# Product-key stages: combining on POOL behind an ACT copy, outputs moved behind the products

## The reference

```
def _L1_ffn_ref(inputs, gamma, beta, w_q, keys, key_in, key_out):   # h=8 heads, nk=32, top 8
    xn = (x - mu) * rsqrt(var + eps) * gamma + beta                  # over all tokens
    q = xn @ w_q.T                                                   # two halves a head
    sim = einsum('pbnhd,hkpd->pbnhk', q, keys)                       # 32 scores a half
    s, i = top_k(sim, 8); all_scores = sx[..., :, None] + sy[..., None, :]
    scores, pk = top_k(all_scores, 8)                                # 8 of 1024 experts a head
    o = einsum('bnd,bnhkd->bnhk', inputs, key_in[idx])
    o = gelu(o) * softmax(scores)
    return einsum('bnhk,bnhkd->bnd', o, key_out[idx])
```

## Time and profile before

| | us |
|---|---|
| median of 3 runs | 1822.73 (1818.83 to 1823.32) |
| the profiled execution | 1822.42 |
| its span | 1820.6 |
| PE busy | 1531.7 (84%) |
| PE weight loads busy | 1234.6 (68%) |
| DVE busy | 1350.5 (74%) |
| ACT busy | 933.3 (51%) |
| POOL busy | 243.7 (13%) |

### The profile page before, as it was taken

How to read it: one execution, slowest core, us unless ns; L and a number is a source line. 1 busy time by engine, 2 the same in 40 slices (tenths; PEclk the granted TensorE clock), 3 DMA queues, 4 the chain that set the end, 5 groups by cost and what they waited for, 6 DMA issues and landing times.

```text
span 1820.6 us, 58068 instructions
## 1 busy us (share of the span) xinstructions
PE 1531.7 (84%) x22876; PEld 1234.6 (68%) x22876; DVE 1350.5 (74%) x4272; ACT 933.3 (51%) x1990; POOL 243.7 (13%) x389
## 2 busy tenths in 40 slices
PE   2767777777579999999986899999958999999995
PEld 1644444445458888888874677777736888888885
DVE  4956666667689999999954556556568899999992
ACT  1814454447375666766722223323336667667670
POOL 2136455432000000000002000000000000000000
PEclk9958898887799999999987899999969999999997
DMA  5000000000011112112110000000001121121212
GB/s 135 1 1 1 1 0 0 0 1 1 0 25 43 40 35 46 35 35 46 35 36 1 1 1 0 0 0 0 0 0 37 36 46 35 36 44 35 45 36 71
DMA packets 27503, 42.67 MB, mean 23 GB/s; under 512 B 6960, under 2 KB 18480, under 8 KB 27440
## 3 DMA queue, kind: packets, MB, share of 16 engines
q1 hardware_dynamic: 27440, 41.82, 10.1%
HBM read 6.15 MB, written 2.10 MB: 5 GB/s over the span
## 4 chain that ended last, share of the span: by engine, by line
PE 48%; DVE 20%; issue 11%; DMA 7%; ACT 5%; SPq 5%; DVEq 2%; POOL 1%; POOLq 0%; ACTq 0%; PEldq 0%
PE bank L1518 19%; DMA rowsD<-work 7%; SPq L305 5%; DVE work L858 4%; DVE work L852 4%; ACT work L941 3%; PE bank L1393 3%; PE bank L1381 3%; PE bank L1430 3%; PE bank L1241 3%; PE bank L1529 2%; PE bank L1165 1%; PE bank L1403 1%; DVE work L582 1%; PE bank L1184 1%
## 5 line engine op out<-in xcount | busy, mean ns | idle before, releaser
L1518 PE MATMUL bank<-rowsD,work 128*32 128x32 f32 x16384 | 366.3, 273 | 48.1 <-DMA rowsD<-work 26.1
L1518 PEld LDWEIGHTS bank<-rowsD,work 128*32 128x32 f32 x16384 | 356.8, 194 | 72.8 <-issue 72.8
L1529 PEld LDWEIGHTS bank<-kout,work 128*128 128x128 f32 x1024 | 252.7, 332 | 26.4 <-issue 19.7
L1529 PE MATMUL bank<-kout,work 128*128 128x128 f32 x1024 | 246.9, 395 | 5.1 <-issue 5.1
L1082 ACT ACT_TABLE_LOAD x62 | 79.5, 1283 | 274.6 <-PE bank L1501 274.6
L1063 ACT ACTIVATE work<-work 128x128 f32<-128x128 f32 x512 | 166.2, 415 | 0.0
L1072 ACT ACTIVATE work<-work 128x128 f32<-128x128 f32 x512 | 157.9, 397 | 0.0
L858 DVE STREAM_TRANSPOSE work<-work 128x1024 f32<-128x1024 f32 x128 | 151.8, 1224 | 8.1 <-DVE work L852 0.3
L330 POOL TENSOR_SCALAR work<-work,gk,bk 128x256 f32<-128x256 f32 x256 | 137.8, 556 | 109.0 <-ACT work L956 109.0
L870 DVE TENSOR_TENSOR work<-bank,work 128x512 f32<-128x512 f32 x128 | 88.0, 692 | 86.7 <-PE bank L1518 82.9
L1020 ACT ACTIVATE work<-bank,work 128x256 f32<-128x256 f32 x128 | 49.8, 481 | 164.8 <-DVE work L716 164.7
(11 more groups left out here) (184 smaller groups left out, 2649.4 us busy)
## 6 DMA issues: line engine op xcount, KB each, us to landing
rowsD<-work SPq DMA_DIRECT2D x256, 128.0 KB, 2.4
x_sb<-in_L_attn_x_dram SPq DMA_DIRECT2D x8, 256.0 KB, 4.5
out_dram<-x_sb SPq DMA_DIRECT2D x4, 512.0 KB, 5.3
headsel<-in_c_headsel_dram SPq DMA_DIRECT2D x1, 512.0 KB, 4.9
work<-in_L_ffn_key_in_dram SPq DMA_DIRECT2D x1, 512.0 KB, 7.8
kout<-in_L_ffn_key_out_dram SPq DMA_DIRECT2D x4, 128.0 KB, 4.5
work<-in_L_ffn_keys_dram SPq DMA_DIRECT2D x1, 256.0 KB, 3.1
wqkv<-in_L_attn_W_qkv_dram SPq DMA_DIRECT2D x1, 192.0 KB, 4.9
```

The source lines that it names most:

```text
L1518: last = nc.tensor.matmul(bank[2 + half][k * NK:(k + 1) * NK, (t % 16) * NK:(t % 16 + 1) * NK], xrows[:, t, :], yrows[:, k, t, :, :], star ...
L1529: last = nc.tensor.matmul(bank[6 + par][:, 0:D], cg[:, par, :].rearrange("p (t j) -> p j t", j=NCH)[:, j, :], kout[:, j, :], start=(j == 0 ...
```

## The change

Three things are changed in the two product-key stages. First, the combining leaves DVE: ACT copies banks 2 and 3 to a new buffer csb (`evacuate`, at the end of each `turn`, for the tile before), and POOL multiplies csb with G5 into cg, in two halves, as soon as DVE's L852 of the next tile is done (semaphore W). Second, the layouts of csb, G5 and cg are turned: products write their 32 columns of PSUM in steps of 64 elements, gelu writes runs of 64, and the weights of `outputs` are 128 adjacent elements of cg, where they were every eighth. Third, on PE `outputs` moves from behind `similarities` to behind `products`, so that a round is similarities(i+2), experts, products(i), outputs(i-1). `products` now waits for ACT's copy (ce) and no more for cg. In the diff the first `combine` is POOL's, the removed one DVE's, `evacuate` and `turn` are ACT's, and the last three pieces PE's; `next_pair` is the old waits and `pair`.

```diff
                 pair(0)
-                with pool.Fori(1, NPAIR) as p:
...
+                next_pair(1)
+                combine(0, 0, 0)
+                next_pair(2)
+                combine(1, 1, 0)
+                with pool.Fori(1, NPAIR // 2 - 1) as q:
+                    for c in range(2):
+                        combine(4 * q - 2 + 2 * c, 0, 1 - c)
+                        next_pair(2 * q + 1 + c)
+                        combine(4 * q - 1 + 2 * c, 1, 1 - c)
...
+                def combine(m, par, gpar):
+                    pool.wait_ge(s["W"], min(base + m + 2, (f + 1) * NT) if isinstance(m, int) else base + m + 2)
+                    pool.wait_ge(s["g"], 4 * NPAIR * f + 2 * (m - par) + 4)
+                    pool.wait_ge(s["ce"], 2 * (base + m) + 2)
...
+                    for half in range(2):
+                        last = nc.gpsimd.tensor_tensor(
+                            cg[:, par, :].rearrange("p (j t) -> p j t", j=NCH)[:, :, half * 64:half * 64 + 64],
+                            csb[:, par, 512 * half:512 * (half + 1)].rearrange("p (j t) -> p j t", j=NCH),
+                            G5[:, gpar, 2 * par + half, :, :], ALU.mult)
+                    last.then_inc(s["cg"], 1)
...
-                def combine(m, par, gpar):
...
-                        nc.vector.tensor_tensor(cg[:, par, c], bank[2 + half][:, :],
...
-                    nc.scalar.activation(G5[:, gpar, :, 2 * u:2 * u + 2],
-                                         bank[4 + u % 2][:, :].rearrange("p (j t) -> p t j", j=2),
+                    nc.scalar.activation(G5[:, gpar, :, 2 * u:2 * u + 2, :].rearrange("p x j t -> p j x t"),
+                                         bank[4 + u % 2][:, :].rearrange("p (j x t) -> p j x t", j=2, x=4),
                                          ACT.Gelu).then_inc(s["g"], 1)
...
+                def evacuate(m, par):
+                    if not (f == 0 and isinstance(m, int) and m < 2):
+                        act.wait_ge(s["cg"], base + m - 1)
+                    for half in range(2):
+                        act.wait_ge(s["tok"], 2 * (base + m) + half + 1)
+                        act.sem_inc(s_go, 1)
+                        nc.scalar.activation(csb[:, par, 512 * half:512 * (half + 1)], bank[2 + half][:, :],
+                                             ACT.Copy).then_inc(s["ce"], 1)
...
                 def turn(p, gpar, u, n):
                     gelu(p, gpar, u)
                     gelu(p, gpar, u + 1)
                     exponentials(n, u // 2)
                     scale(n, u // 2)
+                    evacuate(n - 1, 1 - u // 2)
...
-                            pe.wait_ge(s["cg"], 2 * (base + n) - 1 + half)
+                            pe.wait_ge(s["ce"], 2 * (base + n) - 1 + half)
...
-                                    bank[2 + half][k * NK:(k + 1) * NK, (t % 16) * NK:(t % 16 + 1) * NK],
+                                    bank[2 + half][k * NK:(k + 1) * NK, :]
+                                    .rearrange("p (j t c) -> p t c j", j=NCH, t=16)[:, t % 16, :, :],
...
-                                                cg[:, par, :].rearrange("p (t j) -> p j t", j=NCH)[:, j, :],
+                                                cg[:, par, j * P:(j + 1) * P],
```

More of the change, by code:

```diff
@@ L369, in pair, with next_pair @@
                                             xs5.rearrange("p (a t c) -> p a t c", a=2, c=4), bna[:, 0:1], bnb[:, 0:1], ALU.mult, ALU.add).then_inc(s["zt"], 1)
-                pair(0)
-                with pool.Fori(1, NPAIR) as p:
+                def next_pair(p):
                     pool.wait_ge(s["o"], 4 * (f * NPAIR + p))
@@ L376, in product_keys @@
                     pair(p)
+                def combine(m, par, gpar):
+                    base = f * NT
+                    pool.wait_ge(s["W"], min(base + m + 2, (f + 1) * NT) if isinstance(m, int) else base + m + 2)
+                    pool.wait_ge(s["g"], 4 * NPAIR * f + 2 * (m - par) + 4)
+                    pool.wait_ge(s["ce"], 2 * (base + m) + 2)
+                    if not (f == 0 and isinstance(m, int) and m < 2):
+                        pool.wait_ge(s["y"], base + m - 1)
+                    pool.sem_inc(s_go, 1)
+                    for half in range(2):
[4 more added lines that the diff above has]
+                    last.then_inc(s["cg"], 1)
+                pair(0)
+                next_pair(1)
[7 more added lines that the diff above has]
+                        combine(4 * q - 1 + 2 * c, 1, 1 - c)
+                combine(NT - 6, 0, 1)
+                next_pair(NPAIR - 1)
+                combine(NT - 5, 1, 1)
+                for m in range(NT - 4, NT):
+                    combine(m, m % 2, m // 2 % 2)
             nc.gpsimd.memset(rowsD[:, :, :, :], 0.0).then_inc(pk["dz"], 1)
@@ L860, in rows @@
                                             ).then_inc(s["T"], 1)
-                def combine(m, par, gpar):
[L864 to L869, removed]
-                        nc.vector.tensor_tensor(cg[:, par, c], bank[2 + half][:, :],
-                                                G5[:, gpar, par * P + 64 * half:par * P + 64 * (half + 1), :]
-                                                .rearrange("p t j -> p (t j)"),
-                                                ALU.mult).then_inc(s["cg"], 1)
                 def update(m, par):
@@ L881, in update, with tile @@
                         statistics(m, 1, s, m + 2)
-                def tile(i, par, gpar, ahead=True, back=True, done=True):
+                def tile(i, par, ahead=True, done=True):
                     if ahead:
                         front(i + 1, 1 - par)
-                    if back:
-                        combine(i - 1, 1 - par, gpar)
                     rows(i, par)
@@ L892, in product_keys @@
                 front(0, 0)
[L893 to L900, removed]
+                tile(0, 0, done=False)
+                tile(1, 1, done=False)
+                with dve.Fori(1, NPAIR - 1) as p:
+                    tile(2 * p, 0)
+                    tile(2 * p + 1, 1)
+                tile(NT - 2, 0)
+                tile(NT - 1, 1, ahead=False)
                 update(NT - 2, 0)
@@ L1096, in product_keys @@
                     scale(n, n)
+                    if n:
+                        evacuate(n - 1, 1 - n)
                 with act.Fori(0, NT // 4 - 1) as i:
@@ L1101, in product_keys @@
                 turn(NPAIR - 1, 1, 2, NT - 1)
+                evacuate(NT - 1, 1)
             act.sem_inc(L0["pe"], 2)
@@ L1542, in tile @@
                     products(i, par, pair)
+                    if back:
+                        outputs(i - 1, 1 - par)
                 pe.wait_ge(s["dz"], 1)
```

12 lines of the change are left out of this document (6 added, 6 removed).

## The result

| | before | changed |
|---|---|---|
| median | 1823.03 us | 2074.11 us (2072.45 to 2076.24) |
| ratio | | 1.138, 95% interval 1.137 to 1.140 |
| span of the profiled execution | 1820.6 | 2074.1 |
| PE, DVE, ACT, POOL busy | 84, 74, 51, 13% | 68, 61, 47, 19% |

The change makes the kernel 251 us slower; 299 had been forecast, and 2121 us with a range from 2070 to 2215, so the time lies at its lower end, 11 us under the 2085 to 2157 of the forecast's own mechanism.

A forecast was written before the change was run, and what follows sets the result against it. The kernel was taken as bound by a 13.42 us ring of products, combine, rows and DMA. A new ring of 18.7 us over 30 rounds in each of two stages, with shorter last rounds and longer tails, gave +299: 2121 us, range 2070 to 2215.

The forecast's parts named there:

- the forecast's own mechanism: The ring through ACT's queue sets the pace: 18.1 to 19.3 us a round, 2085 to 2157 us, chance 0.78.
- The ring: Products, ACT's copy, table loads and gelus, exponential of cz, DVE's reduction and rows, DMA, next products: closes in one round.
- The round's length: One turn of the ring in the product-key stages: 18.36 us from its pieces, 18.7 with the clock, against 13.42.
- The clock's 0.35: PE idling about 6.6 us a round gets 1.2 GHz in the products, which adds 0.35 us a round.
- the -0.2 that was allowed: ACT's two gelus, 1.16 to 1.37 us, might be faster with writes in runs: -0.2 to 0 a round.
- The small pieces at L875: Exponential of cz to DVE's reduction ending front, 0.10 us; that reduction and the next instruction, 0.52 us.
- The last rounds: Each stage's last round has no gelu or front behind the copy: about 8.4 us for 13.5, -5.1.
- The tail behind the last products: Copy, two POOL multiplications and outputs at each stage's end: 6.0 us for 4.5, +1.5.
- The costs at nothing: POOL's two multiplications, 3.0 us a tile, and `pair` behind them on POOL hold nobody up: no cost.
- The strided writes into PSUM: Rival: products writing in steps of 64 slow from 5.67 to 9.0 us, +3.3 a round, 2319 us; chance 0.10.
- POOL in DVE's way: Rival: DVE's first transpose waits for a POOL multiplication, +1.5 us a round, 2211 us; chance 0.05.
- The faster case: Rival: copy holds nothing in ACT's queue; the longest ring spans two tiles, 12.5 us a round, 1756 us; chance 0.05.

The follow-up runs named there:

- e1: Changed kernel with ACT's copy of tile n-2 instead of n-1 at the end of turn n: 1754.92 us, ratio 0.962 to the kernel before.
- e2: Changed kernel with two more ACT copies of 128x512 to a spare tile in each turn, behind evacuate: 2135.99 us, against 2074.11 without.
- e4: Changed kernel with banks 2 and 3 copied by DVE, where it combined before, instead of by ACT: 1822.95 us, ratio 1.0005.
- e3: Changed kernel with two more ACT copies of 128x512 in each turn, ahead of evacuate: 2074.21 us, against 2074.11 without.
- e7: Kernel before with the turned layouts alone, DVE combining and PE's order kept: 1816.72 us, ratio 0.998, against 1819.33 in the same session.
- e5: Kernel of e1 with ACT's copy of tile n-2 moved up to right behind the exponential of cz: 1716.73 us, ratio 0.943.

## Why the prediction was right

**The ring** was named with its parts, and it is what the profile shows; e1, e2 and e4 cut it, lengthen it and replace it. e4 gave the time that was expected; e2 gave 62 us for 74, by shorter copies, and e1 missed by 29 us, for which the ring has no term. e3 excludes ACT's load as such.

**The round's length** was put at 18.36 us, and 18.7 with the clock. Measured are 17.9 in the loop, and 18.05 with the first three rounds of each stage. Two terms were mis-sized. The clock's 0.35 is zero: the drop to 1.2 GHz came as said, for the first half of the set, but the sets of the loop take 5.6 to 5.9 us, as before. The longer sets at the ends of the stages had stops in them, and I took part of them for the clock's. The changed kernel has such stops in the first and the last tiles of its stages (171 passes in 3.85 us, then 0.9 of pause), and not in the rounds between; what makes them stays open. The gelus take 1.09 us for two, not 1.37, a little more than the -0.2 that was allowed. The small pieces at L875 (0.38 for 0.52, and 0.03 for the semaphore's 0.10) give another 0.2. Together these are the 0.8 us by which a round of the loop is shorter than the 18.7 of the forecast, 48 us over 60 rounds. What the sum left out went the other way: it gave the rounds at the head of a stage the loop's length, and they are 9 us longer in the two stages together. So the 60 rounds are 39 us under their forecast, and by luck in part.

**The rest of the sum.** The last rounds were close, 8.7 and 8.4 for 8.4. The tail behind the last products was not: put at +1.5 in each stage, it took 11.8 and 11.4 us from the products' start, for 11.4 and 13.0 before, so +0.4 and -1.6, 4 us less together. The forecast of the change, 299 us for 251, was 48 us too large; the 39 of the rounds and these 4 leave 5, which lie mostly outside the two stages, and their cause is open.

**The costs at nothing** held. POOL's two multiplications took 2.52 us for a forecast of 3.0, beside the transposes, and in the loop no engine waited for `pair`. Outputs took 128 ns a pass where 152 were expected, with no effect, as PE idles.

**The rivals.** The strided writes into PSUM cost nothing, 5.73 us for a set; e7 has them in a loop that is 13.4 us long, at 5.5 to 5.8, and there too they show no loss. What the Trainium skill (PSUM — Partial Sum Buffer, Specifications) says of significant slowing is not borne out by these matmuls of 32 columns in four groups of partitions; for wider ones nothing was measured. POOL in DVE's way was nothing in the changed kernel, but became real in e1, by the rule that was cited. The faster case needed another order: 1756 us were worked out for it, and with the copy one turn later e1 gave 1755. That they agree is luck: the ring was put at 12.5 us a round and is 12.0 (e5), and e1's rounds of 12.7 have in them some 0.7 us, the contention most likely, that had been put at nothing.

## What to carry to other kernels

Moving work to an idle engine puts a wait into that engine's queue, and everything behind the wait inherits it: list what stands behind, and follow it until it comes back to what is waited for. If it comes back within one round, and is longer than the other rings, its length is the new pace, however idle the engines are; doing the moved work one round later, when its input is long there, cut the ring here. Once it is cut, look at what runs beside the moved work: here POOL's multiplication cost nothing beside DVE's transposes, with one input in SBUF, and held up an addition with two.

## What the runs showed of the hardware

The matmuls of 128x32 come 22 ns apart at 1.2 as at 2.4 GHz (138 in 2.99 us at a granted 0.50, 256 in 5.62 us at 1.00 in the kernel before). Sixteen passes of 128x128 with adjacent weights took 2.05 us, 128 ns each; with weights in steps of 8 elements one took 241. A DVE addition of 128x64 with two inputs in SBUF took 1.00 us in the mean for 0.22 while POOL multiplied (e1), and the profile counts all of it as busy.
